# A vision tower's tokenizer loop: the first stage runs one half unit further ahead, and two of four doubling transfers become ScalarE copies

## The reference

```python
x = (x - mean) / (1e-06 + std) / sqrt(P)
x = conv2d(x, conv1_w, conv1_b)            # 3 -> 64 channels, 3x3
residual = x
x = gelu(group_norm(x, gn1_g, gn1_b))      # 32 groups
x = conv2d(x, rconv1_w, rconv1_b)          # 64 -> 64 channels, 3x3
x = gelu(group_norm(x, gn2_g, gn2_b))
x = residual + conv2d(x, rconv2_w, rconv2_b)
x = conv2d(x, proj_w, proj_b, stride=16)   # one token of 192 numbers per patch
```

## Time and profile before

| what | value |
|---|---|
| median of 3 runs | 2052.86 us (2050.37 to 2054.92) |
| profiled execution | 2055.91 us, span 2054.0 us |
| busy: PE, DVE, ACT, POOL | 1600.1, 1137.2, 849.1, 904.6 us |
| idle time of PE ended by the doubling transfers | 342.7 us, 129 times |
| mean granted TensorE clock | 0.901 of full |

### The profile page before, as it was taken

One profiled execution on the slowest core, in us unless ns is written; L12 is line 12 of the kernel. 1 busy time (PEld: TensorE's weight loads), 2 busy tenths in 40 slices (PEclk: granted clock), 3 DMA queues, 4 the chain that ended last, 5 costly groups with the idle time before them and its releaser, 6 DMA issues. The chain is left out here.

```text
span 2054.0 us, 45856 instructions
## 1 busy us (share of the span) xinstructions
PE 1600.1 (78%) x13776; PEld 1045.2 (51%) x13776; DVE 1137.2 (55%) x4296; ACT 849.1 (41%) x2114; POOL 904.6 (44%) x2183
## 2 busy tenths in 40 slices
PE   7899767768777777777777777777867775798899
PEld 3344333335554555455554555455535554676556
DVE  7533357765666556555665565655555655137350
ACT  1122245554444444444454444444444442033442
POOL 2000057665555545555555555555555552014320
PEclk9999989988999989898998899889988997897899
DMA  5623433334333333243333333333333337630000
GB/s 156 190 82 99 177 78 75 75 77 104 99 91 85 95 101 94 71 105 94 93 83 92 95 102 86 91 93 95 88 86 95 102 92 194 157 68 1 1 1 12
DMA packets 120759, 188.63 MB, mean 92 GB/s; under 512 B 22839, under 2 KB 90614, under 8 KB 120462
## 3 DMA queue, kind: packets, MB, share of 16 engines
q1 hardware_dynamic: 120590, 186.41, 34.2%
HBM read 103.06 MB, written 19.69 MB: 60 GB/s over the span
## 5 line engine op out<-in xcount | busy, mean ns | idle before, releaser
L500 PE MATMUL rc<-sb_acts,sb_rwd 128*64 128x512 f16 x1764 | 649.7, 445 | 343.1 <-DMA sb_acts<-sb_hst 342.7
L501 PE MATMUL rc<-sb_acts,sb_rwd 128*64 128x512 f16 x1764 | 650.8, 446 | 0.0
L415 ACT ACTIVATE sb_f32q<-c,sb_gsh,sb_gsc 128x128 f32<-128x128 f32 x788 | 297.0, 457 | 578.5 <-POOL sb_gsh L369 578.5
L500 PEld LDWEIGHTS rc<-sb_acts,sb_rwd 128*64 128x64 f16 x1764 | 192.7, 124 | 475.4 <-DMA sb_acts<-sb_hst 392.3
L358 POOL TENSOR_TENSOR sb_tmp<-sb_mst 128x4 f32<-128x4 f32 (+1 forms) x296 | 84.6, 286 | 737.8 <-DVE sb_mst L784 737.8
L363 POOL TENSOR_TENSOR sb_tmp<-sb_tmp,sb_half_neg 128x4 f32<-128x4 f32 (+1 forms) x296 | 386.4, 1306 | 23.2
L500 PE MATMUL rc<-sb_acts,sb_rwl 128*64 128x512 f16 x1176 | 367.3, 394 | 4.3 <-issue 3.9
L501 PE MATMUL rc<-sb_acts,sb_rwl 128*64 128x512 f16 x1176 | 366.9, 394 | 0.0
L424 ACT ACTIVATE sb_g2f<-rc,sb_gsh,sb_gsc 128x128 f32<-128x128 f32 x784 | 296.6, 469 | 164.5 <-POOL sb_gsh L369 153.1
L556 PE MATMUL pj<-sb_wall,sb_arena 128*64 128x384 f16 x1792 | 315.2, 355 | 20.9 <-DMA sb_wall<-w_lo 11.9
L784 DVE TENSOR_REDUCE sb_mst<-st 128x8 f32<-128x16 f32 (+1 forms) x296 | 52.5, 177 | 477.5 <-PE st L544 477.2
(11 more groups left out here) (161 smaller groups left out, 2308.9 us busy)
## 6 DMA issues: line engine op xcount, KB each, us to landing
sb_acts<-sb_hst SPq DMA_DIRECT2D x788, 78.8 KB, 2.1
sb_wall<-w_lo SPq DMA_DIRECT2D x56, 528.0 KB, 4.1
sb_im<-x_planes SPq DMA_DIRECT2D x300, 60.7 KB
sb_wall<-w_lo SPq DMA_DIRECT2D x28, 480.0 KB, 3.7
sb_im<-x_planes SPq DMA_DIRECT2D x300, 30.3 KB
sb_f32q<-in_proj SPq DMA_DIRECT2D x12, 576.0 KB, 4.0
sb_arena<-in_proj SPq DMA_DIRECT2D x12, 576.0 KB, 4.6
w_lo<-sb_arena SPq DMA_DIRECT2D x1, 6144.0 KB, 18.5
```

The lines of the kernel that those rows point to most:

```text
L415: ins = nc.scalar.activation(g1f[:, q * Q + m, :], c1[q][:, m * HALF:(m + 1) * HALF], ACT.Gelu, bias=gsh[q][:, m:m + 1], scale=gsc[q][:, m ...
L500: nc.tensor.matmul(out[0:CH, :], w_odd, x_odd, start=(n == 0), stop=(n == 14))
L501: yield nc.tensor.matmul(out[CH:128, :], w_even, x_even, start=(n == 0), stop=(n == 14))
```

## The change

Five edits belong together. (1) `conv1`, the statistics, `gelu1` and `split1` run one half further ahead: in slot k DVE splits half k+2 instead of k+1, PE does `conv1` of half k+4, and so on; one more half is done ahead of the loop. (2) Of the four transfers of `double`, the two whose source and destination are the same 64 partitions become two ACT copies (`keep`), placed at the start of the ACT slot, for half k+1. The two that cross the partitions stay. (3) PE waits for both kinds: 32 for the transfers and a new semaphore `hi_kept`. (4) `x_planes` gets 18 planes instead of 12 (the first six once more), and `load_im` becomes two requests of 54 rows instead of six of 24 and 12; the rows of the small weights follow. (5) Ahead of the loop this adds one store to `x_planes`, five short zero stores, and ten small requests that place `w1s`.

```diff
-            for h in range(2):
-                sp.dma_start(bass.AP(tensor=scr, offset=h * 6 * PLANE, ap=[[7 * PAD, ROWS], [PLANE, 6], [1, 7 * PAD]]),
+            for k, h in enumerate((0, 1, 0)):
+                sp.dma_start(bass.AP(tensor=scr, offset=k * 6 * PLANE, ap=[[7 * PAD, ROWS], [PLANE, 6], [1, 7 * PAD]]),
                              xhl[:, 6 * h:6 * h + 6, :]).then_inc(s_scr, 16)
...
             def load_im(u, p):
-                for kx in range(3):
-                    sp.dma_start(im[p][24 * kx:24 * kx + 24, 0:RUN],
...
+                for up in range(2):
+                    sp.dma_start(im[p][54 * up:54 * up + 54, 0:RUN],
+                                 bass.AP(tensor=scr, offset=u * (U * PAD) + up * WD,
+                                         ap=[[1, 3], [PLANE, 18], [1, RUN]])).then_inc(s_im[p], 16)
...
                 sp.wait_ge(s_sp1h, k + 1)
-                for row, half in ((0, 0), (0, 1), (1, 1), (1, 0)):
+                for row, half in ((1, 0), (0, 1)):
...
-                        sp.wait_ge(s_c1, 2 * u + 3)
-                        load_im(u + 2, p)
-                        double(2 * u + 1, p, 1)
+                        sp.wait_ge(s_c1, 2 * u + 5)
+                        load_im(u + 3, 1 - p)
                         double(2 * u + 2, 1 - p, 0)
+                        double(2 * u + 3, 1 - p, 1)
...
+            def keep(k, p, q):
+
+                act.wait_ge(s_sp1h, k + 1)
+                for half, row in ((1, 1), (0, 0)):
+                    ins = nc.scalar.activation(acts[p][64 * half:64 * half + 64, row, q * Q * PAD + WD:(q + 1) * Q * PAD],
+                                               hst[q][64 * half:64 * half + 64, WD:Q * PAD], ACT.Copy)
+                ins.then_inc(s_keep, 1)
...
-                            gelu1(2 * u + 1 + q, 1 - q, not (first and p == 0 and q == 0))
+                            keep(2 * u + 1 + q, p if q == 0 else 1 - p, 1 - q)
+                            gelu1(2 * u + 2 + q, q)
...
-                pe.wait_ge(s_dup[p][q], 64 * (pairs_done + 1))
+                pe.wait_ge(s_dup[p][q], 32 * (pairs_done + 1))
+                pe.wait_ge(s_keep, 2 * u + q + 1)
                 woven(1)
-                means(0, N1[q], 2 * u + q + 2, u - (q == 0) if k2 else 0)
+                means(0, N1[1 - q], 2 * u + q + 3, u - (q == 0) if k2 else 0)
...
-                pe.wait_ge(s_g1, 2 * u + q + 2)
-                conv1(1 - q, 1 - p if q == 0 else p)
+                pe.wait_ge(s_g1, 2 * u + q + 3)
+                conv1(q, p)
...
-                    read_means(0, N1[q], k + 2)
-                    if q == 0:
-                        split1(k + 1, 1, p, (pair_at + p) if n2 else None)
-                    else:
-                        split1(k + 1, 0, 1 - p, pair_at + 1)
+                    read_means(0, N1[1 - q], k + 3)
+                    split1(k + 2, q, 1 - p, pair_at + 1)
```

More of the change, by code:

```diff
@@ L37 @@
 RUN = (U - 1) * PAD + 8 * WD + P
-PLANE = (NPAT + 2 * U + 1) * PAD
-KA, KC = 72, 108
+PLANE = (NPAT + 3 * U + 1) * PAD
+KC = 108
 WS = 64.0
@@ L69, in build_front @@
 def build_front(nc, a, emb, xs, ts, wrd):
-    scr = nc.dram_tensor("x_planes", (12, PLANE), F16)
+    scr = nc.dram_tensor("x_planes", (18, PLANE), F16)
     wlod = nc.dram_tensor("w_lo", (128, HALF * E), F16)
@@ L174, in build_front @@
         s_g1, s_sp1h, s_sp1 = sem("gelu1_done"), sem("split1_hi"), sem("split1_done")
-        s_rowz = sem("first_rows_zeroed")
+        s_rowz, s_keep = sem("first_rows_zeroed"), sem("hi_kept")
         s_dup = [[sem(f"hi_doubled{p}{q}") for q in range(2)] for p in range(2)]
@@ L220, in _ @@
             sp.wait_ge(s_wprep, W_READY)
-            sp.dma_start(w1s[0:KA, :], w1hl[0:KA, 0, :]).then_inc(s_w1s, 16)
-            sp.dma_start(w1s[KA:KC, :], w1hl[KA:KC, 1, :]).then_inc(s_w1s, 16)
+            for at in range(0, KC, 18):
+                sp.dma_start(w1s[at:at + 12, :], w1hl[at:at + 12, 0, :]).then_inc(s_w1s, 16)
+                sp.dma_start(w1s[at + 12:at + 18, :], w1hl[at + 12:at + 18, 1, :]).then_inc(s_w1s, 16)
             def fold_io(i, p, last):
@@ L261, in _ @@
                     fold_io(i, p, False)
-            sp.wait_ge(s_scr, 16 * 8)
+            sp.wait_ge(s_scr, 16 * 14)
             load_im(0, 0)
@@ L303, in _ @@
             double(0, 0, 0)
+            sp.wait_ge(s_c1, 3)
+            load_im(2, 0)
+            double(1, 0, 1)
             over_groups(sp, group)
@@ L335, in _ @@
             sp.wait_ge(s_emb, 32 * GROUPS + 32)
-            sp.wait_ge(s_dup[0][0], 64 * (UNITS // 2 + 1))
+            for q in range(2):
+                sp.wait_ge(s_dup[0][q], 32 * (UNITS // 2 + 1))
+            sp.wait_ge(s_im[0], 32 * (UNITS // 2 + 2))
             sp.wait_ge(s_wr, 32)
@@ L373, in pair @@
                     u = u0 + p
-                    norm(0, 0, 2 * u + 2)
+                    norm(0, 1, 2 * u + 3)
                     if not (first and p == 0):
                         norm(1, N2[1 - p], u - 1)
-                    norm(0, 1, 2 * u + 3)
+                    norm(0, 0, 2 * u + 4)
             pool.wait_ge(s_padz, 3)
@@ L381, in _ @@
             norm(0, 1, 1)
+            norm(0, 0, 2)
             over_groups(pool, lambda g, b, first: over_units(pool, g, pair, first))
@@ L456, in _ @@
             gelu1(0, 0, False)
+            gelu1(1, 1, False)
+            keep(0, 0, 0)
             group(0, 0, True)
@@ L632, in _ @@
             pe.sem_inc(s_pj, 1)
-            pe.wait_ge(s_w1s, 32)
+            pe.wait_ge(s_w1s, 192)
             pe.wait_ge(s_rowz, 4)
-            pe.wait_ge(s_im[0], 96)
+            pe.wait_ge(s_im[0], 32)
             pe.wait_ge(s_tev, 3 * FU)
@@ L641, in _ @@
             means(0, 1, 1, 0)
-            pe.wait_ge(s_im[1], 96)
+            pe.wait_ge(s_im[1], 32)
             pe.wait_ge(s_g1, 1)
             conv1(0, 1)
+            means(0, 0, 2, 0)
+            pe.wait_ge(s_g1, 2)
+            conv1(1, 1)
             over_groups(pe, group)
-            means(1, N2[1], UNITS - 1, 2 * UNITS + 2)
+            means(1, N2[1], UNITS - 1, 2 * UNITS + 3)
             for c in range(NCH):
@@ L755, in _ @@
             dve.wait_ge(s_padz, 3)
-            dve.wait_ge(s_scr, 16 * 8)
+            dve.wait_ge(s_scr, 16 * 14)
             v.sem_inc(s_rd[0], 1)
@@ L790, in split1 @@
                 if doubled is not None:
-                    dve.wait_ge(s_dup[1 - p][q], 64 * doubled)
+                    dve.wait_ge(s_dup[1 - p][q], 32 * doubled)
+                    dve.wait_ge(s_keep, k - 1)
                 src = g1f[:, q * Q:q * Q + Q, :].rearrange("p g (r w) -> p g r w", w=P)
@@ L812, in slot @@
                     n2 = not (first and p == 0 and q == 0)
-                    dve.wait_ge(s_c1, k + 4)
-                    channel_stats(0, N1[q], c1[q], 0)
-                    moments(0, N1[q], 7 * (k + 2) + 4)
+                    dve.wait_ge(s_c1, k + 5)
+                    channel_stats(0, N1[1 - q], c1[1 - q], 0)
+                    moments(0, N1[1 - q], 7 * (k + 3) + 4)
                     if n2:
@@ L864, in _ @@
             split1(0, 0, 0, None)
+            dve.wait_ge(s_c1, 4)
+            channel_stats(0, 0, c1[0], 0)
+            moments(0, 0, 7 * 2 + 4)
+            read_means(0, 0, 2)
+            split1(1, 1, 0, None)
             group(0, 0, True)
@@ L881, in _ @@
             dve.wait_ge(s_pj, GROUPS)
-            dve.wait_ge(s_sp1, K + 1)
+            dve.wait_ge(s_sp1, K + 2)
             dve.wait_ge(s_sp2, K + 2)
@@ L1539, in layout @@
                 par, up = dy % 2, dy // 2
-                rows = [kx * 24 + (6 * k + 2 * c + par) * 2 + up for k in range(2)] + [KA + kx * 12 + (2 * c + par) * 2 + up]
+                rows = [up * 54 + kx * 18 + 6 * k + 2 * c + par for k in range(3)]
                 for half in range(2):
```

18 lines of the change are left out of this document (7 added, 11 removed).

## The result

The changed kernel takes 1856.87 us (median of 4 runs, 1847.22 to 1861.16) against 2053.89 us for the kernel before on the same chip: a ratio of 0.9028, 95% interval 0.898 to 0.9075, some 197 us less. The prediction said 1817, range 1790 to 1871. Its profiled execution took 1854.66 us, span 1852.8. One run of the experiments, of e9, took 3687.76 us, counts as a slow one and is left out.

A forecast was written before the change was run, and what follows sets the result against it. PE's wait for doublings, late by SP's queue, bound the kernel; next came the ring through both norms, 12.25 us a pair. 2055.9 - 253.0 (loop) + 11 (front) + 6 (tokens) = 1819.9 profiled, 1817 as median; range 1790 to 1871.

The forecast's parts named there:

- the ring: Main loop: `read_means`, both POOL norms, `gelu2_at`, `hi2`, `split2`, back to `read_means`; 12.14 us a pair, taken as 12.25.
- My own case: Whole kernel: ring of 12.14 to 12.39 us, front of 4 to 14; 1799 to 1834, widened to 1795 to 1840; chance 0.64.
- the copies' ring: Loop rival: ring through `hi2`, second norm, ACT copies and `gelu1`, 10.45 us plus copies; 1846 to 1871 us, chance 0.18.
- Loop with the tokens: Main loop: 98 pairs of 12.25 us, 1200.5 us, plus 6 us for DVE reading tokens at group ends.
- POOL beside DVE: First norm's gsc operation on POOL slows from 0.26 to 0.51 us beside `split2`; about 0.25 a pair, middle taken: 12.25.
- The front: Before the loop: added stores to `x_planes` and zero stores on SP delay a staged load, +11 us, at most 13.7.
- Behind the last cast: Stretch after the loop's last cast: 349 us, claimed untouched by the change.
- The copies: ACT copies of 64x630 in the loop: about 0.74 us each, 1.6 a slot with the wait, up to 2.1.
- What bounds the kernel now: Main loop before the change: PE waits for doubling transfers, 342.7 us in 129 waits; 14.83 us a pair.
- Late by SP's queue: Main loop: one half in two has transfers delayed by SP's requests, 13.3 us for 14 a pair.
- Signs: Expected in the changed loop: DVE waits for `hi2` some 1 us each, PE idle before group sums 1.5 us a pair.

The follow-up runs named there:

- e9: The changed kernel with both DVE differences (remainders of both stages) made one-operand copies, so low halves hold rounded values: 1783.38 us, ratio 0.866.
- e1: The changed kernel with all four doublings as transfers again and no ACT copies; lead and large loads stay: 1846.52 us, ratio 0.8972.
- e2: The changed kernel with the second stage's means read ahead of `split2` in the q = 0 slot: 1877.78 us, ratio 0.9142.
- e3: The changed kernel with `split2` run one slot later, for half k-4 instead of k-3: 1794.12 us, ratio 0.8715.
- e3b: e3 with all four doublings by transfers and no copies on ACT: 1759.46 us, ratio 0.8579.

## Why the prediction was right, and where it was off

The mechanism was right: transfers off PE's path, DVE waiting for `hi2`, and the pair set by the ring that the earlier trace rows show closed once. That the time lies in the range is in part luck. My own case ended at 1840; 1856.87 is covered only by the part of the range that was taken in for the copies' ring, and e1 shows that this ring did not set the pace. Against the profiled execution the sum was 1819.9, and 1854.7 came, 34.8 more; two other errors, of 6.5 us each, cancel by chance. By its terms:

- *Loop with the tokens.* Predicted 1200.5 + 6, measured 1241.3: 34.8 too little. The mis-sized term is the section "POOL beside DVE". It let only `split2` meet the first norm's gsc product, and took 0.11 of 0.25 us a pair. It didn't ask where the cast and difference of `split1` go when DVE's wait for PE ends. They went into the second norm, at 0.4 us a pair on average. The walked ring is 12.55 and not 12.25, 29 us of the 34.8; 3.2 more are the extra half ahead of the loop (from the first cast at 255.9 to the second at 259.1), which the sum left out. The ends of the stretched operations show the meeting, and that e2 loses some 20 us by one more of its kind shows that it is on the path; e9 shows the same, for the first norm above all.
- *The front.* Predicted +11. The stores to `x_planes` grew from 11.1 to 20.3 us on SP, the fold step behind them waited 14.07 for 9.06, and it started at 101.70 for 96.48: +5.2. The stores took 9.2 us more, not the 13.7 allowed, and less of that came through. The first cast is 4.5 us later, 6.5 less than predicted.
- *Behind the last cast.* Predicted unchanged at 349; it is 355.6, 6.5 more. No run explains it: over all the traces here this stretch takes 342 to 361 us.
- *The copies.* 733 ns each for an estimated 740; from their start to `gelu1`'s 1.39 behind the second norm, for the 1.6 allowed. The rival of the copies' ring was refuted by e1, but e3 and e3b show that it is the next ring.
- *What bounds the kernel now.* "Late by SP's queue" was half true. Fewer loads alone gave 106 of some 200 us, since the loads stand ahead of the doubling that is wanted; but SP had work for 10.9 of 14.83 us a pair, and 13.3 us for 14 requests counted a wait as work. The forecast didn't suffer, since it needed only that the wait goes.
- *Signs.* DVE's wait for `hi2` came as one of 3.11 and one of 0.34 us a pair, not 1 in each slot. PE's idle time before the sums is 0.74 and 0.23 in the pair shown, for 1.5, and another wait of 0.96, for `gelu2_at`, was not forecast.

## What to carry to other kernels

When a wait goes, ask of each operation that stood behind it where it lands now, and beside which engine's work; the ring's own lengths may change by the move. Walk the next ring from a stretch where it is already closed, then look for the third one before you cut the second: here 12.6, 12.1, 11.7 and 11.4 us a pair followed one another. Of parts that serve one end, time each alone: here the lead without the other two was the fastest of the combinations run.

## What the runs showed of the hardware

GpSimd's small operations of 0.20 us took 0.4 to 0.7 when they met a VectorE difference of 512 columns from two SBUF tiles; the loss depends on which operation meets it, and here it was worth some 20 us (e2) to 47 (e9) of 1857. The Trainium skill (SBUF — State Buffer, who interferes with whom) tells of a port pair that both engines share as an exclusive lock. The rows agree: the 294 stretched operations all end 0.05 to 0.07 us behind the VectorE operation that they met. A VectorE copy with one SBUF input left the 128x8 product at 384 ns on average, between 202 and 596. The same section says that a cast or copy can hold the pair too, when it runs in a two-port mode. That the casts from fp32 to fp16 hold GpSimd up is shown by e9, where 115 operations end in the same way behind one; no run here tells in which mode they ran.

The granted TensorE clock in the loop was higher with PE's shorter waits. The windows view gives per stretch the engines' busy time, then the clock; before:

```profile
300.00:1700.00 1400.00, 1054.24 (x10208) 714.80 (x10208) 843.42 (x3493) 677.05 (x1693) 790.53 (x1977) 0.90 0.35 91
```

and after:

```profile
300.00:1497.00 1197.00, 971.96 (x10252) 689.03 (x10254) 833.18 (x3520) 943.07 (x2084) 778.50 (x1985) 0.99 0.29 81
```

PE is busy 75% of the first stretch at 0.90 of full and 81% of the second at 0.99, means over the clock's two levels, 1.2 and 2.4 GHz. What the clock alone was worth was not separated.
